# Spreading the router and preparation of the next chunk over all 34 slots of a chunk, with a fused sum of the picked scores

## The reference

```python
scores = jax.nn.sigmoid(logits)
sfc = scores + correction_bias[None, :]
grp = sfc.reshape(T, G, E // G)
top2, _ = jax.lax.top_k(grp, 2)
group_scores = top2.sum(-1)
_, gidx = jax.lax.top_k(group_scores, TOPK_GROUP)
...
masked = jnp.where(emask > 0, sfc, 0.0)
_, tidx = jax.lax.top_k(masked, K)
tw = jnp.take_along_axis(scores, tidx, axis=1)
tw = tw / (tw.sum(-1, keepdims=True) + 1e-20)
```

## Time and profile before

| | us |
|---|---|
| median of 3 runs | 572.5 (572.01 to 573.7) |
| the profiled execution: its time | 574.56 |
| its span, first to last instruction | 572.8 |
| busy: PE, DVE, ACT, POOL | 508.6, 496.0, 470.4, 469.3 |
| DMA | 149.32 MB, mean 261 GB/s |

### The profile page before, as it was taken

One profiled execution on the slowest core, in us unless ns is written; L12 is line 12 of the kernel. 1 busy time (PEld: TensorE's weight loads), 2 busy tenths in 40 slices (PEclk: granted clock), 3 DMA queues, 4 the chain that ended last, 5 costly groups with the idle time before them and its releaser, 6 DMA issues.

```text
span 572.8 us, 7918 instructions
## 1 busy us (share of the span) xinstructions
PE 508.6 (89%) x1666; PEld 278.0 (49%) x1666; DVE 496.0 (87%) x1158; ACT 470.4 (82%) x922; POOL 469.3 (82%) x430
## 2 busy tenths in 40 slices
PE   2158899998898988999899998999989998999996
PEld 1034445554454545565455544555445554555552
DVE  3657899899988899899998899888998899979984
ACT  2768798799886998888986998879988889988872
POOL 2389898897888979897988978889897979968762
PEclk9999999999999999999999999999999999999999
DMA  8956865887869877987678877697769877699951
GB/s 200 326 166 229 277 258 197 318 291 259 247 191 348 276 261 232 347 271 262 247 239 307 304 264 248 197 364 264 272 216 321 300 249 246 219 318 353 317 189 37
DMA packets 65649, 149.32 MB, mean 261 GB/s; under 512 B 14048, under 2 KB 31040, under 8 KB 65600
## 3 DMA queue, kind: packets, MB, share of 16 engines
q1 hardware_dynamic: 63728, 147.07, 76.3%
q10 hardware_dynamic: 1872, 1.75, 0.9%
HBM read 143.03 MB, written 5.77 MB: 260 GB/s over the span
## 4 chain that ended last, share of the span: by engine, by line
POOL 28%; issue 22%; DVE 18%; PE 14%; ACT 8%; DMA 8%; SPq 1%; POOLq 1%; DVEq 0%; ACTq 0%
POOL yacc L546 10%; DMA bc_rows<-bc_dram 7%; PE DN L1088 7%; POOL bc_rows L537 6%; DVE DC L944 4%; DVE relu L885 4%; POOL xn L444 3%; DVE g L831 3%; DVE bc_rows L897 3%; PE U L1038 2%; PE U L1039 2%; PE U L1040 2%; ACT act L715 2%; POOL rstd L438 1%; POOL rest L527 1%
## 5 line engine op out<-in xcount | busy, mean ns | idle before, releaser
L1088 PE MATMUL DN<-act,down 128*128 128x512 f32 x512 | 261.9, 593 | 1.9 <-ACT act L715 1.9
L715 ACT ACTIVATE act<-relu 128x512 f32<-128x512 f32 x272 | 169.5, 623 | 44.6 <-DVE relu L885 38.3
L885 DVE SCALAR_TENSOR_TENSOR relu<-U,gate_rows 128x512 f32<-128x512 f32 x256 | 173.6, 678 | 34.0 <-PE U L1040 17.8
L546 POOL TENSOR_TENSOR yacc<-yacc,bc_rows 128x512 f32<-128x512 f32 x120 | 154.5, 1287 | 44.9 <-DVE bc_rows L897 44.9
L1038 PE MATMUL U<-x_hi,up_hi 128*128 128x512 f32 x256 | 163.4, 638 | 23.5 <-DVE relu L885 22.5
L537 POOL TENSOR_TENSOR bc_rows<-dtx_all,bc_rows 128x512 f32<-128x512 f32 x128 | 164.4, 1285 | 20.2 <-DMA bc_rows<-bc_dram 20.2
L944 DVE TENSOR_TENSOR_SCAN DC<-DC,carry,bc_rows 128x512 f32<-128x512 f32 x96 | 122.7, 1278 | 0.0
L1088 PEld LDWEIGHTS DN<-act,down 128*128 128x128 f32 x512 | 95.3, 188 | 28.7 <-ACT act L715 6.6
L1038 PEld LDWEIGHTS U<-x_hi,up_hi 128*128 128x128 f32 x256 | 48.2, 188 | 113.7 <-DVE relu L885 70.1
L1039 PE MATMUL U<-x_lo,up_hi 128*128 128x512 f32 x256 | 101.2, 395 | 0.0
L1040 PE MATMUL U<-x_hi,up_lo 128*128 128x512 f32 x256 | 101.1, 395 | 0.0
(11 more groups left out here) (113 smaller groups left out, 501.5 us busy)
## 6 DMA issues: line engine op xcount, KB each, us to landing
bc_rows<-bc_dram SPq DMA_DIRECT2D x128, 512.0 KB, 6.0
gate_rows<-gate_dram SPq DMA_DIRECT2D x128, 512.0 KB, 4.8
xs<-in_L_attn_x SPq DMA_DIRECT2D x8, 256.0 KB, 5.6
down<-in_L_ffn_down_w SPq DMA_DIRECT2D x8, 256.0 KB, 4.9
xr<-in_L_attn_x SPq DMA_DIRECT2D x8, 256.0 KB, 5.6
rest_kept_dram<-rest SPq DMA_DIRECT2D x8, 256.0 KB, 4.3
out<-res SPq DMA_DIRECT2D x8, 256.0 KB, 4.5
dtx_all<-in_L_ffn_up_w SPq DMA_DIRECT2D x3, 512.0 KB, 5.6
```

The source lines that it names most:

```text
L546: g.tensor_tensor(yacc[:, :], yacc[:, :], c_rows[:, (c * N + n) % BUFS, :], ALU.add).then_inc(yacc_done, 1)
L715: a.activation(act_at(c, slot), relu[:, slot % 2, :], ACT.Square).then_inc(sq_done, 1)
L885: v.scalar_tensor_tensor(out=relu[:, slot % 2, :], in0=U[slot % 2][:, :], scalar=0.0, in1=gate_rows[:, k // 2 % SBUFS, slot % 2, :], op0=A ...
L1088: mm(DN[:, :], w, act_at(c, slot), start=slot == 0, stop=slot == SLOTS - 1).then_inc(down_done, 1)
```

## The change

It moves nearly every piece of `prep` to another slot. A new function `due(c, slot)` says which pieces stand in a slot. The numbers of the pieces now run from -5 to 28: the pieces -5 to -1 (statistics, `rstd`, `xn`) of chunk `c + 2` stand in the last five slots of chunk `c`, the rest in slots 0 to 28 of chunk `c + 1`. In chunk 0 the pieces of chunk 1 start late and are caught up in slots 21 to 24. `xn` of chunk 1 is now made by DVE instead of POOL, and POOL's `xn` is cut in two halves. `out_mm` and `result` of the chunk before go from slots 19 and 20 to 11 and 12. SP loads the next `xs` later in the chunk, and each `gate_rows` load one state later. On DVE, the product of `picked` and `sig` and its sum, two instructions for all four blocks of tokens, become four instructions that do both, one for each block of 64 columns.

```diff
-        DVE_PREP = 11
+        DVE_PREP = 10
+        EARLY = 5
...
+        def due(c, slot):
+            if c == 0:
+                if slot < 21:
+                    mine = [slot - 3] if slot else list(range(-EARLY, -2))
+                elif slot < 24:
+                    mine = [2 * slot - 24, 2 * slot - 23]
+                else:
+                    mine = [slot]
+                mine = [(1, p) for p in mine if p < SLOTS - EARLY]
+            else:
+                mine = [(c + 1, slot)] if slot < SLOTS - EARLY else []
+            if slot >= SLOTS - EARLY:
+                mine.append((c + 2, slot - SLOTS))
+            return [(pc, p) for pc, p in mine if pc < NCH]
...
                 for n in range(N):
-                    if n == 0 and not last:
-                        x_next(c)
+                    if n == 5 and c + 2 < NCH:
+                        x_next(c + 1)
...
-                    if n:
-                        gates_in(c, n - 1)
+                    if n > 1:
+                        gates_in(c, n - 2)
+                gates_in(c, N - 2)
                 gates_in(c, N - 1)
...
-                if slot == 2 and pc:
-                    pool.wait_ge(rstd_ready, pc + 1)
-                    wait(pool, lgt_done, pc)
-                    alone(pool)
-                    for k in range(KB):
+                if slot in (-2, -1) and pc > 1:
+                    if slot == -2:
+                        pool.wait_ge(rstd_ready, pc + 1)
+                        wait(pool, lgt_done, pc)
+                        alone(pool)
+                    for k in range(KB // 2) if slot == -2 else range(KB // 2, KB):
                         i = g.tensor_scalar(xn[:, k, :], xs[:, k, :], mv[:, k, 0:1], rstd[:, k:k + 1],
                                             ALU.subtract, ALU.mult)
-                    i.then_inc(xn_ready, 1)
+                    if slot == -1:
+                        i.then_inc(xn_ready, 1)
...
-            RECIP_AT = {10: [0, 1], 11: [2, 3]}
+            RECIP_AT = {8.5: [0], 9: [1], 9.5: [2], 10: [3]}
...
-                if slot == 3 and pc == 0:
-                    dve.wait_ge(rstd_ready, 1)
+                if slot == -2 and pc <= 1:
+                    dve.wait_ge(rstd_ready, pc + 1)
+                    wait(dve, lgt_done, pc)
...
-                if slot == 22:
+                if slot == 25:
                     dve.wait_ge(picked_ready, pc + 1)
-                    ch.then(v.tensor_tensor(masked[:, :, :], picked[:, :, :], sig[:, :, :], ALU.mult))
-                if slot == 22.5:
-                    ch.wait()
-                    v.tensor_reduce(wsum[:, :], masked[:, :, :], axis=AX.X, op=ALU.add).then_inc(wsum_ready, 1)
+                    for k in range(KB):
+                        i = v.scalar_tensor_tensor(out=masked[:, k, :], in0=picked[:, k, :], scalar=1.0, in1=sig[:, k, :],
+                                                   op0=ALU.mult, op1=ALU.mult, accum_out=wsum[:, k:k + 1])
+                    i.then_inc(wsum_ready, 1)
...
-                if slot == 4:
+                if slot == 1:
                     pe.wait_ge(xn_ready, pc + 1)
...
-                if slot == 26:
+                if slot == 28:
                     pe.wait_ge(cc_ready, pc + 1)
```

More of the change, by code:

```diff
@@ L431, in prep @@
             def prep(pc, slot):
-                chain = chains["p"]
-                if slot == 1:
+                chain = chains[pc]
+                if slot == -3:
                     pool.wait_ge(var_ready, pc + 1)
@@ L560, in chunk @@
                     main(c, slot)
-                    if not last:
-                        prep(c + 1, slot)
-                assert last or chains["p"].n == POOL_PREP, chains["p"].n
-            chains["p"] = Chain(pool, pool_prep, 0)
-            for slot in range(SLOTS):
-                if slot == 12:
+                    for pc, p in due(c, slot):
+                        prep(pc, p)
+                assert last or chains[c + 1].n == POOL_PREP, chains[c + 1].n
+            for pc in range(NCH):
+                chains[pc] = Chain(pool, pool_prep, pc * POOL_PREP)
+            for slot in range(-EARLY, SLOTS - EARLY):
+                if slot == 11:
                     pool.wait_ge(w_late, 5 * 16)
@@ L732, in chunk @@
                     main(c, slot)
-                    if not last:
-                        prep(c + 1, slot)
-            for slot in range(SLOTS):
-                if slot == 7:
+                    for pc, p in due(c, slot):
+                        prep(pc, p)
+            for slot in range(-EARLY, SLOTS - EARLY):
+                if slot == 5:
                     constants()
-                if slot in (12, 18, 22, 26):
-                    split_up((12, 18, 22, 26).index(slot))
-                if slot == 24:
+                if slot in (11, 17, 21, 24):
+                    split_up((11, 17, 21, 24).index(slot))
+                if slot == 21:
                     act_e.wait_ge(dve_init, 3)
@@ L842, in prep @@
                     op(v.memset, gtop[:, :, TOPG:], 3.0e38)
-                if slot == 17:
-                    ch.wait(True)
-                    for k in range(KB):
+                if slot in (17, 18):
+                    if slot == 17:
+                        ch.wait(True)
+                    for k in range(KB // 2) if slot == 17 else range(KB // 2, KB):
                         groups = slice(k * G, (k + 1) * G)
@@ L925, in chunk @@
                         norms(c - 1)
-                    if not last:
-                        prep(c + 1, slot - 0.5)
-                    if slot == 20 and not first:
+                    for pc, p in due(c, slot)[:1]:
+                        prep(pc, p - 0.5)
+                    if slot == 12 and not first:
                         result(c - 1)
@@ L1125, in chunk @@
                         down_mm(c, 0)
-                    if slot == 19 and not first:
+                    if slot == 11 and not first:
                         out_mm(c - 1)
-                    if not last:
-                        prep(c + 1, slot)
+                    for pc, p in due(c, slot):
+                        prep(pc, p)
             def out_mm(c):
```

109 lines of the change are left out of this document (56 added, 53 removed).

## The result

The changed kernel takes **587.15 us** (median of 4 runs, 586.96 to 589.58), the kernel before, run beside it, 572.58 (572.01 to 573.7): a ratio of 1.0262, 95% interval [1.0231, 1.0293]. It is slower by 2.6%. The forecast was 582, the range 560 to 591. The profiled execution has a span of 587.6 against 572.8, so there are 14.8 us to place.

A forecast was written before the change was run, and what follows sets the result against it. PE was taken to set the pace, with DVE nearly full in slots 9 to 22. Six chunks +6.0, chunk 0 +1.0 and prologue +2.7 gave +9.7 us: 584.3 profiled, 582 us median, range 560 to 591.

The forecast's parts named there:

- A chunk: Chunks 1 to 6: the terms -1.0 - 1.3 - 0.3 + 1.9 + 1.0 + 0.3 + 0.4 give +1.0 us each.
- The fused four: DVE, end of slot 25: four fused instructions alternate with POOL's, 2.7 us in place of 1.26 + 0.41, plus 1.0 a chunk.
- `picked` +0.3 and `g1c` +0.4: DVE in each chunk: these instructions meet POOL's work and wait for it, adding 0.3 and 0.4 us.
- The wait for `xn` in slot 1: PE, end of slot 1: `xn` ready at 375.4, needed at 373.45, so PE waits 1.9 us every chunk.
- The sum of POOL's work: POOL, from `yacc` of slot 26 to the end of `xn`: 16.8 us of instructions to issue.
- Waits that go: Per chunk: DVE's waits for the sigmoid and `sfc` go, -1.0 us; PE's wait for `xn` in slot 4, -1.3.
- the -0.3 for the spreading: DVE pieces moved to slots 23 to 33 and 0 to 8, where PE is the bound: minus 0.3 us a chunk.
- Chunk 0: Waits of 2.5 and 0.6 us go; DVE's `xn` of chunk 1 adds 1.2 + 1.2 (0 to 5), other terms 1.7: +1.0.
- Prologue: Before chunk 0: `masked` starts 2.6 us later behind `rootq`, may be 0.8 shorter; fused four and `cc` add 0.9: +2.7.
- Rival 3: Gate store and loads come late, DVE waits at slot 3 another 1.5 us a chunk: 591 us; chance 0.13.
- Rival 1: Fused four's turn-taking or POOL's lateness with `xn` is absent, each 1.9 us a chunk: 570 us; chance 0.25.
- Rival 2: Levelling pays in full, `xn` reaching PE within 16.2 us; chunk falls to PE's 63.1 plus 0.4: 557 us; chance 0.20.

The follow-up runs named there:

- experiment 1: Changed kernel with the fused sum taken back to one multiplication (slot 25) and one reduction (start of slot 26): 576.75 us, ratio 1.0074.
- Experiment 6: On the changed kernel, `vare`, `rstd`, `xn` one slot earlier: 587.07 us. On experiment 1's kernel, POOL's `rest` product in slot 14 instead of 28: 570.95 us.
- experiment 5: Changed kernel with POOL also making `xn` of chunk 1, DVE only that of chunk 0: 585.09 us, ratio 1.0223.
- experiment 3: Changed kernel with the four fused operations in slot 25 reading one input from PSUM (results not the reference's): 574.86 us, ratio 1.0061.
- experiment 4: Experiment 1's kernel with both operations in slot 25 and the reduction made five times, holding up `relu` as long as the fused form: 587.13 us.

## Why the prediction was right, and where it was not

The sign, the range and the sum for a chunk held; the sum's parts less so.

- **A chunk: +1.0 forecast, +1.1 measured.** Without the fused form it is -0.5, where my other terms made 0.0; the fused form is +1.6, where I had +1.0. Two errors of half a microsecond met, and that the sum came out so close is luck.
- **The fused four.** Forecast: 1.9 us of waiting for the product and `cc`, 0.2 each, 2.7 in all. Measured: 2.2 in all (231.24 to 233.40), behind just those two instructions. The term was still too small because of what the four replaced: the two operations, put in this place (experiment 1), hold DVE for 0.32 us each from start to start, 0.64 together, not for the 1.67 of the earlier trace rows, since the product does not have to wait for POOL there. 2.2 less 0.64 is 1.5, the term had 1.0, and the chunk shows 1.6. What I had nowhere is the **clock**. I treated TensorE's idle time as lost time only; 2.7 us of it brought 1.2 GHz for some microseconds, which made chunk 3, the dearest of the six, 4.3 us longer than the same chunk of experiment 1, of which 1.9 is the stall (2.72 less 0.85). On the mean of six chunks this does not show: TensorE's matmuls take 7.0 us more than in experiment 1 (busy time of chunks 1 to 6), but its waits for `xn` in slot 1 are 6.0 us less, because POOL catches up behind a low clock. So the clock explains why the chunks are uneven, and not the 1.6.
- **`picked` +0.3 and `g1c` +0.4.** Right: means of 786 and 716 ns in place of 418 and 300.
- **The wait for `xn` in slot 1, 1.9.** 1.6 behind chunks at full clock, and hardly any behind a chunk with a low clock. The sum of POOL's work was right: 16.8 us from the `yacc` of slot 26 to the end of `xn` were forecast, and chunk 2 of the changed kernel took 16.7 (234.75 to 251.44). Experiment 6 confirms the cause from one side: 1.04 us less of work took 1.0 off the wait. That an order with all of `xn` further ahead would not help is not shown.
- **Waits that go, -1.0 and -1.3.** They went. The -0.5 of experiment 1 is these two and the -0.3 for the spreading against the wait of slot 1, `picked` and `g1c`; how large each of the three is was not measured apart. One reading behind them was too strong: between chunks 2 and 3 of the kernel before, 2.4 us apart, TensorE's wait for `xn` makes up only 1.63.
- **Chunk 0, +1.0; measured +5.4.** This is the step that failed, in size. "Up to four waits for POOL, I take 1.2" priced them as if POOL had only short instructions there; three of the four waited, one of them for the splitting of weights, 2.59. The four took 5.31, 2.9 more than the term, and taking them away gave 3.0. A part of the 3.0 is the low clock, which stood at 0.50 for some 10 us in the changed kernel and not at this place in experiment 5. The fused form is another 2.6 (75.93 - 73.30), where 1.7 stood for it and `picked` and `g1c`. The bound of 5 was in the working and should have been nearer to the value taken.
- **Prologue, +2.7; measured +2.8, for a reason told only in part.** The end came near 36 as forecast. I had nearly all of it from `masked` behind `rootq`, but with that order taken back and `dtx_all` still ahead of `cc` nothing was gained; with both taken back 2.5 to 2.8. So `masked` was not enough by itself; the order of `dtx_all` and `cc` was never taken back alone, and whether that is enough stays open.
- **Rivals.** Rival 3 (gates late) did not occur: no `relu` waits for a DMA. Rival 1, one cost absent, would have needed the form of experiment 3; with one cost gone the time is 574.9 to 576.8, not 570. Rival 2 did not occur either: the wait in slot 1 is 1.6, and DVE's slot 25 takes 4.6. The time came near it, 559.7 against 557, only with the sum in two operations, `rest` in another slot, `xn` off POOL and the prologue's order restored, and even then a chunk takes 64.5, not the 63.5 of its sum. (Its 16.2 us for `xn` are counted from 357.25. From 358.6, where POOL's 16.8 begin, to 373.45 there are 14.9.)

## What to carry to other kernels

Before fusing DVE operations, look at where their inputs lie and what POOL does at that moment: n short instructions with two SBUF inputs can wait n times, one long one waits once, and one with an input in PSUM not at all. When an engine is late at the end of a loop, taking work out of that stretch helps (1.0 us for 1.04 here); another order helps only if less work stands ahead of what is waited for. And a stall of TensorE of 2 to 3 us in a full stretch can have a lower clock behind it: here this made single chunks up to 4.3 us longer, while another engine that had been late caught up, so that the mean hardly moved. Ask who catches up before adding it.

## What I had not expected of the hardware

- One stall of 2.5 to 2.7 us, nearly the same in every chunk, brings the granted clock down to 0.50 behind it in some chunks only (4 of chunks 1 to 6 in the changed kernel, 3 in experiment 4); where it does not, matmuls take 0.40 us as ever. What decides it stays open. (TensorE: Matmul & The Clock Gate, in the Trainium skill, section on what is actually happening, has these two levels and a clock that depends on how busy TensorE was.)
- A `tensor_scalar` of DVE with one SBUF tensor and per-partition scalars (`xn`, 128x128) also takes turns with POOL: 342 ns on average in the prologue of the kernel before, where POOL was idle, and 5.31 us for four beside POOL's two products and its splitting of weights. So it is not only a second tensor input that does it. The reductions of experiment 4, one SBUF input each, did not wait (1.40 us for four, beside POOL). The Trainium skill, on the page and in the section on interference named above, agrees with both: it lists `tensor_scalar` among the operations that can enter a mode with both ports, and says that `tensor_reduce` never contends on this chip.
- Reading out an accumulated sum is an instruction of its own, 0.08 us, and overlaps the next one: four fused instructions with one PSUM input took 0.56 us.
